# First layer of a graph network: VectorE's block in another order, and half of the products of exponentials and source rows made by GpSimd

## The chip, the cores and the metric

The kernel runs on 1 core of one Trainium2 chip. Its engines are TensorE (PE in the profile, PEld for its weight loads), VectorE (DVE), ScalarE (ACT), GpSimd (POOL) and SyncE (SP), which issues most DMAs. The metric is the device time of one execution in microseconds; less is better. A time stands for the median of several runs.

## The reference

Four graph layers follow each other on 6250 nodes of 16 features, each with a residual and a layer norm; the edges are 200,000, sorted by their target node. Only the first layer is touched by the change. For each edge and each of 16 x 16 pairs (input feature, output feature) it takes a softmax over the edges of a target, and sums the messages with it:

```
w_m = (efeat @ W_msg + b_msg).reshape(E, in_f, -1)
w_a = (efeat @ W_attn + b_attn).reshape(E, in_f, -1)
h_src = feat[src][:, :, None]
e1 = w_m * h_src
e2 = w_a * h_src
seg_max = segment_max(e2, dst)
ex = exp(e2 - seg_max[dst])
denom = segment_sum(ex, dst)
attn = ex / denom[dst]
ft = segment_sum(e1 * attn, dst)
return ft.sum(axis=1)
```

with efeat the 16 edge attributes and dst the sorted targets. Since every edge has 256 values here, this layer works on 200,704 x 256 floats (edges filled up to 128 x 1568).

## The kernel before

**Tiling.** Partition p holds the edges 1568 p to 1568 p + 1567. A block is 8 successive edges of every partition (TB0 = 8, a tile of 128 x 8 x 256), and 196 blocks follow each other (NB0 = 196). Blocks are handled in turns: `loop` writes the first turns out, then runs a hardware loop whose body holds U0 = 4 blocks (buffers b.k = 0 to 3), then writes the last ones out. Every engine has its own instruction list in an order written out by hand, and they meet through semaphores. `b.on(-1)` is the block before b; in the bodies a is b.on(-1) and c is b.on(-2), so that in one turn VectorE works on three blocks at three stages. `at(q)` puts edge q in slot 2 (q % 4) + q // 4 of a tile; a half is four slots.

**The steps of a block**, with their lines in the profile:
- GpSimd gathers the 8 source rows h of each partition, one indirect DMA for each (`gather`, L606), after SyncE has loaded the indices and the edge attributes (`load_in`, L551).
- TensorE multiplies attributes and weights: `weigh(b, half, 0)` gives w_a of a half and `weigh(b, half, 1)` w_m (L627). Each kind has one PSUM tile of a half's size, so the second half is multiplied when VectorE has read the first.
- VectorE makes e2 = w_a * h (`logits`, L702), a running maximum forward over the 8 edges (`forward`, L716) and back again (`backward`, seven steps, L724), and `factor` (L731), the logarithm of what the sums carried in from the block before are scaled by.
- TensorE puts e2 into PSUM (`put_back`, L635) and subtracts the maxima there (`less_maxima(b, n)`, n = 3 to 0, L639). Slots 4 to 7, the second half, take n = 3 and 2.
- ScalarE takes the exponentials of each half from PSUM into PX[:, 0] (`exp_half`, L680, 128x1024) and of the factor (L684).
- The product of the exponentials and h goes into PX[:, 1]. VectorE makes slots 0 to 3 with one instruction (`exp_by_source`, L740, semaphore l_t); ScalarE makes slots 4 to 7 with 64 instructions of 16 columns, each with a scale of its own (L690, semaphore l_x).
- VectorE multiplies this by w_m (`messages(b, half)`, L760), scales the sums carried in (`carried`, L750) and adds up step by step (`sum_step`, eight, L767 and L770). ST holds the denominators and numerators, and SyncE stores it and the maxima M.

**What sets the order around the change.** `weigh(c, 1, 1)` waits until `messages(c, 0)` has read the PSUM tile (semaphore l_p). TensorE does its list in order, so a's `less_maxima` that stand behind `weigh(c, 1, 1)` also wait for it. `exp_half(a, 0)` waits for `less_maxima(a, 0)`, and this for all seven `backward` steps of a. `put_back(b, n)` waits for `exp_half(a, .)`, which reads the same banks. A GpSimd gather into h[b.k] waits until the products of block b-4 have read that buffer. `search_pool` adds 49 gathers between those of the four blocks before the last four, and `search_pool_2` 49 more (L469) at the end of GpSimd's list for the layer; `search_vector_2` on VectorE waits for these.

## Time and profile before

| | us |
|---|---|
| median of 3 runs | 12024.61 |
| lowest and highest | 12020.43 and 12028.92 |
| profiled execution, its span (first to last instruction) | 11300.0 |
| VectorE busy in the span | 9347.3 (83%) |
| TensorE busy in the span | 9392.3 (83%) |
| ScalarE busy in the span | 8259.4 (73%) |
| GpSimd busy in the span | 7314.2 (65%) |

The profiled execution is known by its span alone; what a run takes outside the span (launch and end) is not in the trace, and the medians of the runs hold it. The first layer ends near 3890 us; the other three layers fill the rest. A duration in the trace is that of one instruction; where one engine's instructions overlap at their ends, the distance of two starts says what one costs.

### The profile page before, as it was taken

The page shows a single profiled execution, that of the slowest core. Times are in us where ns is not written, and L with a number is a line of the kernel's source. Part 1 is how long each engine was busy: PE and PEld are TensorE (multiplying, and loading weights), DVE is VectorE, ACT ScalarE, POOL GpSimd, SP SyncE. Part 2 cuts the span into 40 slices and gives each one's busy share as a digit, 9 for nine tenths or more (in the row PEclk, how much of TensorE's full clock was granted, in tenths as well). Part 3 has the DMA queues.
Part 4 walks back from the last instruction along what each step waited for, and adds up shares of the span by engine and source line. Part 5 has one row for each costly group of instructions (what it writes and reads, how often), then busy time and mean ns, then how long its engine had stood idle before and what let it go on. Part 6 is the DMA issues. An engine that isn't in the chain of part 4 may idle for free. (4 is left out here: it accounts for less than half of the span.)

```text
span 11300.0 us, 166457 instructions
## 1 busy us (share of the span) xinstructions
PE 9392.3 (83%) x41198; PEld 6666.9 (59%) x41198; DVE 9347.3 (83%) x14740; ACT 8259.4 (73%) x16314; POOL 7314.2 (65%) x6233
## 2 busy tenths in 40 slices
PE   5888888888888408997999488888799979988997
PEld 2333333333333206776888377777688858876886
DVE  8999999999999697886555499999587858776876
ACT  4777777777777406885888288888488848875885
POOL 4555555555555626776777677777277757776776
PEclk7666666666666559998999699999799979998998
DMA  3444444444444328886999211111299969987995
GB/s 123 178 176 176 177 178 177 176 178 178 178 178 177 126 83 293 300 304 205 287 286 287 53 48 45 46 45 45 81 331 326 330 193 328 328 288 234 330 327 190
DMA packets 756442, 2256.46 MB, mean 200 GB/s; under 512 B 278617, under 2 KB 426734, under 8 KB 679886
## 3 DMA queue, kind: packets, MB, share of 16 engines
q10 hardware_dynamic: 161280, 1027.68, 25.2%
q1 hardware_dynamic: 394718, 984.91, 25.2%
q0 software_dynamic: 200304, 242.20, 9.3%
q8 instruction: 64, 1.05, 0.0%
q14 instruction: 76, 0.62, 0.0%
HBM read 1321.84 MB, written 932.33 MB: 199 GB/s over the span
## 5 line engine op out<-in xcount | busy, mean ns | idle before, releaser
L606 POOL DMA_INDIRECT h<-in_x,idx x1568 | 2062.7, 1315 | 1672.8 <-DMA efT<-in_edge_attr_t 1236.5
L690 ACT ACTIVATE PX<-PX,h 128x16 f32<-128x16 f32 x12544 | 2509.6, 292 | 6.4
L639 PE MATMUL PS<-M,minus_ident 128*128 128x512 f32 x1568 | 1419.8, 1032 | 311.7 <-DVE M L724 311.7
L2029 PE MATMUL PS<-mhr,lhs 128*128 128x392 f32 x6272 | 1249.7, 355 | 194.9 <-DVE lhs L2193 194.9
L1996 POOL DMA_INDIRECT myg<-node_table,mix x784 | 1134.5, 1447 | 397.7 <-issue 235.7
L2092 ACT ACTIVATE mhr<-mhb 128x1568 fp32r<-128x1568 bf16 x784 | 1142.0, 1505 | 276.3 <-DVE mhb L2183 246.6
L2029 PEld LDWEIGHTS PS<-mhr,lhs 128*128 128x128 f32 x6272 | 1144.2, 192 | 276.5 <-ACT mhr L2092 217.8
L627 PE MATMUL PS<-waug,efT 17*128 17x256 f32 x6272 | 1043.1, 534 | 317.5 <-DVE e L702 291.3
L1509 PEld LDWEIGHTS PS<-every_weight,dstf 128*128 128x128 f32 x8960 | 1214.5, 190 | 137.4 <-DVE dstf L1641 38.9
L1509 PE MATMUL PS<-every_weight,dstf 128*128 128x144 f32 (+1 forms) x8960 | 1243.9, 282 | 27.3 <-DVE dstf L1641 26.9
L627 PEld LDWEIGHTS PS<-waug,efT 17*128 17x128 f32 x6272 | 612.9, 252 | 1050.5 <-issue 483.9
L770 DVE SCALAR_TENSOR_TENSOR ST<-ST,flb,PX 128x512 f32<-128x512 f32 x1372 | 1021.5, 745 | 1.4
L1560 ACT ACTIVATE r0hot<-r0hb 128x3584 fp32r<-128x3584 bf16 x224 | 716.9, 3201 | 383.5 <-DVE r0hb L1628 286.9
L1483 POOL DMA_INDIRECT c0yg<-node_table,c0ix x672 | 723.6, 1077 | 406.2 <-POOLq L1832 201.6
L680 ACT ACTIVATE PX<-PS 128x1024 f32<-128x1024 f32 x392 | 396.7, 1012 | 756.9 <-PE PS L639 756.9
L639 PEld LDWEIGHTS PS<-M,minus_ident 128*128 128x128 f32 x1568 | 397.3, 294 | 847.6 <-DVE M L724 518.5
L1483 POOL DMA_INDIRECT r0yr<-node_table,r0ix x672 | 747.1, 1112 | 230.9 <-issue 156.4
L1483 POOL DMA_INDIRECT c2yg<-node_table,c2ix x672 | 722.6, 1075 | 245.9 <-issue 185.4
L1483 POOL DMA_INDIRECT c1yg<-node_table,c1ix x672 | 720.8, 1073 | 246.6 <-issue 186.6
L1560 ACT ACTIVATE r1hot<-r1hb 128x3584 fp32r<-128x3584 bf16 x224 | 716.1, 3197 | 205.1 <-PE PS L1499 115.8
L1483 POOL DMA_INDIRECT r1yr<-node_table,r1ix x672 | 688.9, 1025 | 229.6 <-issue 182.3
L1560 ACT ACTIVATE c0hot<-c0hb 128x3584 fp32r<-128x3584 bf16 x224 | 716.3, 3199 | 135.0 <-PE PS L1499 93.3
(436 smaller groups left out, 20636.5 us busy)
## 6 DMA issues: line engine op xcount, KB each, us to landing
softmax_maxima<-M SPq DMA_DIRECT2D x196, 1024.0 KB, 3.9
softmax_denominators<-ST SPq DMA_DIRECT2D x196, 1024.0 KB
softmax_numerators<-ST SPq DMA_DIRECT2D x196, 1024.0 KB
one_hot_rows_of_sources<-r0hb ACTq DMA_DIRECT2D x224, 896.0 KB
r1hb<-one_hot_rows_of_sources ACTq DMA_DIRECT2D x224, 896.0 KB
c0hb<-one_hot_rows_of_sources ACTq DMA_DIRECT2D x224, 896.0 KB
c1hb<-one_hot_rows_of_sources ACTq DMA_DIRECT2D x224, 896.0 KB
c2hb<-one_hot_rows_of_sources ACTq DMA_DIRECT2D x224, 896.0 KB
```

Of the source, the lines that this page charges most:

```text
L606: PO.indirect_dma_start(h[b.k][:, at(q), :], None, io["x"], bass.IndirectOffsetOnAxis(ap=idx[b.k][:, q:q + 1], axis=0))\
L627: mm = PE.matmul((wm if message else wa)[:, at(q) - 4 * half, :], efT[b.k][row:row + D + 1, q // 4, :], waug[row:row + D + 1, C2 * message ...
L639: mm = PE.matmul(PS[0:CH, 4 + n, :], minus[:, :], M[b.k % 2][:, n::4, :], start=False, stop=True)
L680: S.activation(PX[b.k][:, 0, 4 * half:4 * half + 4, :], below[:, 4 * half:4 * half + 4, :], ACT.Exp).then_inc(l_ex, 1)
L690: act = S.activation(PX[b.k][:, 1, t, D * i:D * i + D], PX[b.k][:, 0, t, D * i:D * i + D], ACT.Copy, scale=h[b.k][:, t, i:i + 1])
L770: V.scalar_tensor_tensor(out=s[:, :, q, :], in0=s[:, :, q - 1, :], scalar=flb[b.k][:, q, 1:2], in1=P[:, :, at(q), :], op0=ALU.mult, op1=AL ...
L1483: PO.indirect_dma_start(to, None, table, bass.IndirectOffsetOnAxis(ap=ix[b.k][:, q:q + 1], axis=0))\
L1509: mm = PE.matmul(weighed(q)[:, r, 0:R * D], mx[q % (1 + LAG)][:, 128 * r:128 * r + 128], every[:, 0:R, :].rearrange("p r o -> p (r o)"))
L1560: S.activation(hot_[q % 2][:, :, :], hb[q // 2 if make else q % 4][:, q % 2 if make else 0, :, :], ACT.Copy)\
L1996: PO.indirect_dma_start(yg[b.k][:, q, :], None, table8, bass.IndirectOffsetOnAxis(ap=ix[b.k][:, q:q + 1], axis=0)).then_inc(m_g[b.k], 16)
L2029: mm = PE.matmul(PS[:, 6 + k, 0:A7 // 2], lhs[(G * b.k + q) % 2][:, 2 * two + r, part, :], hr[(2 * G * b.k + j) % 4][:, r, k * A7 // 2:(k ...
L2092: S.activation(hr[at_][:, :, :], hb[at_][:, :, :], ACT.Copy).then_inc(c_wd, 1)
```

## The change

VectorE's turn is written in another order: all seven backward steps of a stand in it, from its start on, where four stood at the end of the turn before; `messages(c, 0)` stands behind five of them, and `factor(a)` behind `forward(b, 0)`. `carried` moves to the turn of c. `exp_by_source` moves from VectorE to GpSimd, just ahead of the gathers into the same buffer, and makes slots 4 to 7; ScalarE's 64 products make slots 0 to 3. ScalarE takes the factor's exponential behind those of the halves. TensorE takes `less_maxima(a, 3)` behind `weigh(b, 0, 0)` and `less_maxima(a, 2)` behind `weigh(c, 1, 1)`. On GpSimd and VectorE two turns are written out ahead of the loop (head = 2).

```diff
@@ -93,13 +93,14 @@
     return not isinstance(count, int) or count > 0
 
 
-def loop(eng, body, n, tb, first=None, last=None, u=2, tail=1):
+def loop(eng, body, n, tb, first=None, last=None, u=2, head=1, tail=1):
 
     if first:
         first(Blk(0, 0, n, tb, u))
-    for k in range(u):
-        body(Blk(0, k, n, tb, u))
-    with eng.Fori(1, n // u - tail) as i:
+    for i in range(head):
+        for k in range(u):
+            body(Blk(i, k, n, tb, u))
+    with eng.Fori(head, n // u - tail) as i:
         for k in range(u):
             body(Blk(i, k, n, tb, u))
     for i in range(n // u - tail, n // u):
@@ -595,6 +596,16 @@
                 SP.wait_ge(l_ms[k], 16 * NB0 // U0)
 
         def l0_pool():
+            def exp_by_source(b):
+                P = PX[b.k]
+                PO.wait_ge(l_ex, b.count(3, 3))
+                PO.nop(nofuse=True)
+                if b.on(1).exists():
+                    PO.wait_ge(l_bw, b.on(1).count(TB0 - 1, 5))
+                PO.tensor_tensor(P[:, 1, OWN:, :].rearrange("p t (i o) -> p t i o", i=D),
+                                 P[:, 0, OWN:, :].rearrange("p t (i o) -> p t i o", i=D),
+                                 bc(h[b.k][:, OWN:, :], D, 3), ALU.mult).then_inc(l_t, 1)
+
             def gather(b):
                 PO.wait_ge(l_in[b.k], b.slot(32, 32))
                 if due(n := b.on(-U0).count(1, 1)):
@@ -609,7 +620,16 @@
                 if isinstance(b.i, int) and b.i == NB0 // U0 - 2:
                     search_pool(range(13 * b.k, min(13 * b.k + 13, JT)))
 
-            loop(PO, gather, NB0, TB0, u=U0, tail=2)
+            def body(b):
+                if b.on(-U0).exists():
+                    exp_by_source(b.on(-U0))
+                gather(b)
+
+            def last(b):
+                for n in range(1 - U0, 1):
+                    exp_by_source(b.on(n))
+
+            loop(PO, body, NB0, TB0, last=last, u=U0, head=2, tail=2)
             search_pool_2()
 
         def l0_tensor():
@@ -630,7 +650,7 @@
 
             def put_back(b, n):
                 PE.wait_ge(l_e2, b.count(2, 2 - n // 2))
-                if due(m := b.on(-1).count(3, 3 - n // 2)):
+                if due(m := b.on(-1).count(3, 2 - n // 2)):
                     PE.wait_ge(l_ex, m)
                 PE.matmul(PS[0:CH, 4 + n, :], ident[:, :], e2[:, 2 * n:2 * n + 2, :], start=True, stop=False)
 
@@ -646,14 +666,13 @@
             def body(b):
                 a = b.on(-1) if b.on(-1).exists() else None
                 c = b.on(-2) if b.on(-2).exists() else None
+                weigh(b, 0, 0)
                 if a:
                     less_maxima(a, 3)
-                weigh(b, 0, 0)
-                if a:
-                    less_maxima(a, 2)
                 if c:
                     weigh(c, 1, 1)
                 if a:
+                    less_maxima(a, 2)
                     less_maxima(a, 1)
                     less_maxima(a, 0)
                 for n in (3, 2, 1, 0):
@@ -680,12 +699,12 @@
                 S.activation(PX[b.k][:, 0, 4 * half:4 * half + 4, :], below[:, 4 * half:4 * half + 4, :], ACT.Exp).then_inc(l_ex, 1)
 
             def body(b):
+                exp_half(b, 1)
+                exp_half(b, 0)
                 S.wait_ge(l_a, b.count(1, 1))
                 S.activation(cf[b.k % 2][:, :], cf[b.k % 2][:, :], ACT.Exp).then_inc(l_ex, 1)
-                exp_half(b, 1)
-                exp_half(b, 0)
                 S.wait_ge(l_ex, b.count(3, 3))
-                for t in range(OWN, TB0):
+                for t in range(OWN):
                     for i in range(D):
                         act = S.activation(PX[b.k][:, 1, t, D * i:D * i + D], PX[b.k][:, 0, t, D * i:D * i + D], ACT.Copy,
                                            scale=h[b.k][:, t, i:i + 1])
@@ -732,19 +751,10 @@
                                        scalar=flb[b.k][:, 0, 0:1], in1=M[b.k % 2][:, 0, :],
                                        op0=ALU.add, op1=ALU.subtract).then_inc(l_a, 1)
 
-            def exp_by_source(b):
-                P = PX[b.k]
-                V.wait_ge(l_ex, b.count(3, 3))
-                if due(n := b.on(-U0).count(TB0, TB0)):
-                    V.wait_ge(l_s, n)
-                V.tensor_tensor(P[:, 1, 0:OWN, :].rearrange("p t (i o) -> p t i o", i=D),
-                                P[:, 0, 0:OWN, :].rearrange("p t (i o) -> p t i o", i=D),
-                                bc(h[b.k][:, 0:OWN, :], D, 3), ALU.mult).then_inc(l_t, 1)
-
             def carried(b):
                 if due(n := b.slot(32, 0)):
                     V.wait_ge(l_st[b.k], n)
-                V.wait_ge(l_ex, b.count(3, 1))
+                V.wait_ge(l_ex, b.count(3, 3))
                 if due(n := b.count(TB0, 0)):
                     V.wait_ge(l_s, n)
                 V.tensor_tensor(ST[b.k][:, :, 0, :], ST[(b.k - 1) % U0][:, :, TB0 - 1, :],
@@ -753,8 +763,9 @@
             def messages(b, half):
                 ts = slice(4 * half, 4 * half + 4)
                 P = PX[b.k]
-                V.wait_ge(l_t, b.count(1, 1))
                 if half:
+                    V.wait_ge(l_t, b.count(1, 1))
+                else:
                     V.wait_ge(l_x, b.count(1, 1))
                 V.wait_ge(l_wm, b.count(2, half + 1))
                 V.tensor_tensor(P[:, 1, ts, :], wm[:, :, :], P[:, 1, ts, :], ALU.mult).then_inc(l_p, 1)
@@ -776,20 +787,28 @@
                 a = b.on(-1) if b.on(-1).exists() else None
                 c = b.on(-2) if b.on(-2).exists() else None
                 if a:
+                    backward(a, 0)
+                if c:
+                    carried(c)
+                if a:
+                    backward(a, 1)
+                logits(b, 1)
+                if a:
+                    backward(a, 2)
+                    backward(a, 3)
                     backward(a, 4)
-                logits(b, 1)
+                if c:
+                    messages(c, 0)
+                logits(b, 0)
                 if a:
                     backward(a, 5)
                 if c:
-                    messages(c, 0)
+                    sum_step(c, 0)
                 if a:
                     backward(a, 6)
-                logits(b, 0)
+                forward(b, 0)
                 if a:
                     factor(a)
-                if c:
-                    sum_step(c, 0)
-                forward(b, 0)
                 if c:
                     sum_step(c, 1)
                 forward(b, 1)
@@ -799,24 +818,17 @@
                     forward(b, q)
                     if c:
                         sum_step(c, q)
-                backward(b, 0)
-                if a:
-                    carried(a)
-                backward(b, 1)
-                backward(b, 2)
-                backward(b, 3)
-                if a:
-                    exp_by_source(a)
                 if isinstance(b.i, int) and b.i == NB0 // U0 - 1 and b.k == 0:
                     search_vector()
 
             def last(b):
-                for n in (4, 5, 6):
+                backward(b, 0)
+                carried(b.on(-1))
+                for n in range(1, TB0 - 1):
                     backward(b, n)
                 factor(b)
                 for c in (b.on(-1), b):
                     if c.k == b.k:
-                        exp_by_source(c)
                         carried(c)
                     messages(c, 0)
                     sum_step(c, 0)
@@ -825,7 +837,7 @@
                     for q in range(2, TB0):
                         sum_step(c, q)
 
-            loop(V, body, NB0, TB0, last=last, u=U0, tail=1)
+            loop(V, body, NB0, TB0, last=last, u=U0, head=2, tail=1)
             search_vector_2()
 
         l0_first_vector()
```

VectorE, one turn inside the written-out start (M is the maxima, e the logits e2, PS PSUM, PX the exponentials and products, ST the sums, cf the factor). Before:

```order
L740 TENSOR_TENSOR PX<-PX,h 128x1024 [waits l_ex]
L724 SCALAR_TENSOR_TENSOR M<-M,flb 128x256 [waits l_bw,l_fw]
L702 TENSOR_TENSOR e<-PS,h 128x1024 [waits l_wa,l_g3]
L724 SCALAR_TENSOR_TENSOR M<-M,flb 128x256 [waits l_bw,l_fw]
L760 TENSOR_TENSOR PX<-PS,PX 128x1024 [waits l_wm,l_t]
L724 SCALAR_TENSOR_TENSOR M<-M,flb 128x256 [waits l_bw,l_fw]
L702 TENSOR_TENSOR e<-PS,h 128x1024 [waits l_wa]
L731 SCALAR_TENSOR_TENSOR cf<-M,flb 128x256 [waits l_q,l_bw]
L767 TENSOR_TENSOR ST<-ST,PX 128x2x256 [waits l_q,l_p]
L716 SCALAR_TENSOR_TENSOR M<-M,flb,e 128x256 [waits l_ms1,l_fw,l_e2,l_fl3]
L770 SCALAR_TENSOR_TENSOR ST<-ST,flb,PX 128x2x256 [waits l_s,l_p]
...
L760 TENSOR_TENSOR PX<-PS,PX 128x1024 [waits l_wm,l_x,l_t]
```

The same turn after (L743 is backward, L721 logits, L771 messages, L760 carried, L735 forward, L750 factor, L778 and L781 the sums):

```order
L743 SCALAR_TENSOR_TENSOR M<-M,flb 128x256 [waits l_bw,l_fw]
L721 TENSOR_TENSOR e<-PS,h 128x1024 [waits l_wa,l_g3]
L743 SCALAR_TENSOR_TENSOR M<-M,flb 128x256 [waits l_bw,l_fw] x3
L771 TENSOR_TENSOR PX<-PS,PX 128x1024 [waits l_wm,l_x]
L721 TENSOR_TENSOR e<-PS,h 128x1024 [waits l_wa]
L743 SCALAR_TENSOR_TENSOR M<-M,flb 128x256 [waits l_bw,l_fw]
L778 TENSOR_TENSOR ST<-ST,PX 128x2x256 [waits l_q,l_p]
L743 SCALAR_TENSOR_TENSOR M<-M,flb 128x256 [waits l_bw,l_fw]
L735 SCALAR_TENSOR_TENSOR M<-M,flb,e 128x256 [waits l_ms1,l_fw,l_e2,l_fl3]
L750 SCALAR_TENSOR_TENSOR cf<-M,flb 128x256 [waits l_q,l_bw]
...
L771 TENSOR_TENSOR PX<-PS,PX 128x1024 [waits l_wm,l_t]
```

The wait on l_x, ScalarE's products, has moved from the second messages of a turn to the first, and the product L740 is gone from VectorE.

TensorE in the written-out start, one turn (L627 is weigh, L639 less_maxima, L635 put_back). Before:

```order
L639 MATMUL PS<-M,minus_ident 128x512 [waits l_bw]
L627 MATMUL PS<-waug,efT 128x256 [waits l_e2,l_in3]
L627 MATMUL PS<-waug,efT 128x256 x3
L639 MATMUL PS<-M,minus_ident 128x512 [waits l_bw]
L627 MATMUL PS<-waug,efT 128x256 [waits l_p]
L627 MATMUL PS<-waug,efT 128x256 x3
L639 MATMUL PS<-M,minus_ident 128x512 [waits l_bw] x2
L635 MATMUL PS<-e,ident 128x512 [waits l_ex,l_e2] x4
```

After (L647, L659 and L655):

```order
L647 MATMUL PS<-waug,efT 128x256 [waits l_e2,l_in3]
L647 MATMUL PS<-waug,efT 128x256 x3
L659 MATMUL PS<-M,minus_ident 128x512 [waits l_bw]
L647 MATMUL PS<-waug,efT 128x256 [waits l_p]
L647 MATMUL PS<-waug,efT 128x256 x3
L659 MATMUL PS<-M,minus_ident 128x512 [waits l_bw] x3
L655 MATMUL PS<-e,ident 128x512 [waits l_ex,l_e2] x4
```

Behind the weigh that waits on l_p three less_maxima stand now, where two stood.

## Rows read from the trace of the kernel before

**Rows 1.** Page, VectorE's tenths; window, busy us of PE, PEld, DVE, ACT, POOL, clock.
```profile
DVE  8999999999999697886555499999587858776876
...
1000.00:3000.00 2000.00, 1704.29 (x5062) 738.71 (x5063) 1925.30 (x3165) 1585.58 (x7063) 1117.63 (x842) 0.68 0.48 177
```

**Rows 2.** Instructions of line L740: count, duration min/median/max, first and last start.
```profile
L740 DVE TENSOR_TENSOR PX<-PX,h x196: 1209/1217/1225, 124.9 to 3859.4; 128x1024 f32<-128x1024 f32 x196
```

**Rows 3.** Timeline of VectorE: start us, duration us, instruction; two blocks far apart.
```profile
504.58 1.22 DVE L740 TENSOR_TENSOR PX<-PX,h 128x1024 f32<-128x1024 f32 x1
...
3499.93 1.22 DVE L740 TENSOR_TENSOR PX<-PX,h 128x1024 f32<-128x1024 f32 x1
```

**Rows 4.** Timeline of VectorE in one block; in brackets the idle time before.
```profile
2003.83 1.21 DVE L702 TENSOR_TENSOR e<-PS,h 128x1024 f32<-128x1024 f32 x1
...
2005.36 1.21 DVE L760 TENSOR_TENSOR PX<-PS,PX 128x1024 f32<-128x1024 f32 x1
2006.49 0.47 DVE L724 SCALAR_TENSOR_TENSOR M<-M,flb 128x256 f32<-128x256 f32 x1
2007.22 1.23 DVE L702 TENSOR_TENSOR e<-PS,h 128x1024 f32<-128x1024 f32 x1 [0.26 <-PE PS L627]
2008.36 0.48 DVE L731 SCALAR_TENSOR_TENSOR cf<-M,flb 128x256 f32<-128x256 f32 x1
2008.76 0.68 DVE L767 TENSOR_TENSOR ST<-ST,PX 128x512 f32<-128x512 f32 x1
...
2011.23 1.23 DVE L760 TENSOR_TENSOR PX<-PS,PX 128x1024 f32<-128x1024 f32 x1 [0.34 <-PE PS L627]
```

**Rows 5.** Timeline of TensorE in the same block and into the next.
```profile
2005.10 2.08 PE L627 MATMUL PS<-waug,efT 17*128 17x256 f32 x8 [1.59 <-DVE e L702]
2007.10 2.08 PE L639 MATMUL PS<-M,minus_ident 128*128 128x512 f32 x2
2009.11 2.08 PE L627 MATMUL PS<-waug,efT 17*128 17x256 f32 x8
2011.12 3.78 PE L639 MATMUL PS<-M,minus_ident 128*128 128x512 f32 x4
2014.69 3.75 PE L635 MATMUL PS<-e,ident 128*128 128x512 f32 x8
...
2030.02 3.78 PE L639 MATMUL PS<-M,minus_ident 128*128 128x512 f32 x4
```

**Rows 6.** Timeline of ScalarE in the same block.
```profile
2009.80 0.40 ACT L684 ACTIVATE cf<-cf 128x256 f32<-128x256 f32 x1
...
2014.94 1.02 ACT L680 ACTIVATE PX<-PS 128x1024 f32<-128x1024 f32 x1 [3.84 <-PE PS L639]
2015.99 12.80 ACT L690 ACTIVATE PX<-PX,h 128x16 f32<-128x16 f32 x64
```

**Rows 7.** Windows of 0.9 us; granted clock third from the end (PEclk).
```profile
2014.40:2015.30 0.90, 0.90 (x3) 0.36 (x2) 0.90 (x3) 0.36 (x1) 0.28 (x1) 0.67 0.92 391
...
2035.10:2036.00 0.90, 0.90 (x3) 0.45 (x2) 0.90 (x2) 0.90 (x6) 0.86 (x1) 0.79 0.49 155
```

**Rows 8.** Timeline of GpSimd, first and last of eight gathers; two other operations by line.
```profile
2015.02 1.43 POOL L606 DMA_INDIRECT h<-in_x,idx  x1 [5.36 <-DMA efT<-in_edge_attr_t]
...
2027.36 0.94 POOL L606 DMA_INDIRECT h<-in_x,idx  x1 [0.30 <-issue]
...
L1939 POOL IOTA iob<- 128x784 int16 x1 | 0.8, 782 | 0.0
...
L281 POOL TENSOR_SCALAR_AFFINE_SELECT tn<-tn 128x128 f32<-128x128 f32 x1 | 0.3, 289 | 0.0
```

**Rows 9.** End of the layer: L469's gathers by line; VectorE's timeline.
```profile
L469 POOL DMA_INDIRECT lasts_got<-in_dst,search_at x49: 943/947/4532, 3814.0 to 3885.0; - x49
...
3861.11 1.22 DVE L760 TENSOR_TENSOR PX<-PS,PX 128x1024 f32<-128x1024 f32 x1
...
3887.29 1.79 DVE L489 TENSOR_TENSOR lasts_got<-lasts_got,tn 128x1568 f32<-128x1568 int32 x1 [13.85 <-DMA lasts_got<-in_dst,search_at]
```

## The prediction, made before the changed kernel ran

> **What bounds the kernel now.** I read the page's row of busy tenths first: VectorE stands at 9 in the first fourteen slices of forty, which are the first layer [rows 1]. The change touches nothing else. Then the period: VectorE's product L740 runs once per block, 196 times [rows 2]; from its start at 504.58 to its start at 3499.93 us there are 158 blocks, so one block takes 2995.35 / 158 = 18.96 us [rows 3]. From 1000 to 3000 us VectorE is busy for 1925 of 2000 us [rows 1]; the idle times that recur in a block are 0.26 and 0.34 us, both ahead of a product that reads a PSUM tile of TensorE [rows 4]. VectorE is thus the bound, and its instructions fill the block.
>
> The timelines of ScalarE and TensorE show how near the next bound is. What follows names, in VectorE's turn for block b, a = b-1 and c = b-2, as the code does. From the start of messages(c, 0) at 2005.36 [rows 4] the chain goes: weigh(c, 1, 1) on TensorE at 2009.11, which must overwrite the PSUM tile that messages(c, 0) has read; less_maxima(a, 1) and (a, 0) from 2011.12 [rows 5]; the exponentials of a's first half at 2014.94; 64 small products from 2015.99, which last 12.80 us and end at 2028.79 [rows 6]. In the kernel before these products belong to the second half and are wanted by messages(a, 1), at about 2030.2 (one period after the 2011.23 of [rows 4]). So a chain of 23.4 us ends 1.4 us before it is needed, because its consumer comes 5.87 us (2011.23 - 2005.36) later in the turn than the instruction that starts it. I rest the forecast on this number.
>
> **What the change does, part by part.**
>
> 1. VectorE loses L740. Its duration is 1.217 us [rows 2], of which about 1.13 us count, as a product of that size lets the next instruction start 1.13 us after it (2005.36 to 2006.49, [rows 4]). Worth 1.13 us per block while VectorE is the bound: 196 x 1.13 = 221 us. The rest of VectorE's list has the same instructions. The new order also puts three steps of the backward pass and messages(c, 0) between logits(b, 1) and logits(b, 0), and this removes the wait of 0.26 us; the 0.34 goes too, as more work stands between the two messages.
>
> 2. ScalarE makes the products of the first half (t = 0 to 3) in place of the second. Same count, 64 of 128x16, same 12.80 us. But now messages(c, 0) waits for them, and messages(c, 0) itself starts the chain that leads to the next ones. The cover of 5.87 us is gone: the chain closes on itself in one turn, and its length is a lower bound of the period, whatever VectorE saves.
>
> 3. TensorE: weigh(b, 0, 0) goes ahead of less_maxima(a, 3), which is harmless, as both are done while the chain is elsewhere. less_maxima(a, 2), which stood ahead of weigh(c, 1, 1), goes behind it, so that the chain holds three of these matmuls where it held two.
>
> 4. The length of the new chain, from the start of messages(c, 0), with TensorE at 1.2 GHz:
> to the start of weigh(c, 1, 1) 1.27 us (2003.83 to 2005.10, a VectorE product of that size and the matmuls that wait for it, [rows 4, 5]);
> weigh to the first less_maxima 2.01 (2009.11 to 2011.12, [rows 5]);
> one more less_maxima 1.71: the two at 2011.12 hold four records, and their ends let the next group start 3.57 us later at 2014.69, which with the switch of weights is 0.86 for each of the two records of one [rows 5];
> the last two, to the start of the exponentials 3.82 (2011.12 to 2014.94, [rows 5, 6]);
> the exponentials 1.0 (1.05 to the next start), then the carried factor's exponential, which now stands here, 0.40, and 0.05 for the wait on its completion [rows 6];
> 64 products 12.80 [rows 6];
> back to VectorE 0.07, taken as the 0.06 from the end of a VectorE instruction at 2005.04 to TensorE's start at 2005.10.
> Sum 1.27 + 2.01 + 1.71 + 3.82 + 1.45 + 12.80 + 0.07 = 23.13 us.
> It does not help that backward(a, 6) is early enough: after messages(c, 0) come logits 1.14, backward 0.40 (the distance that steps of 256 elements have, 2008.36 to 2008.76), the first sum 0.68 and backward(a, 6) 0.48 [rows 4], so it ends at 1.13 + 2.70 = 3.83 us at the latest, well ahead of the last less_maxima.
>
> 5. TensorE's clock. The granted clock is 0.50 (1.2 GHz) at the weigh, less_maxima and weigh of [rows 5], and becomes 1.00 (2.4 GHz) at about 2015.0 in one block and 2035.5 in the next [rows 7], 3.9 and 5.5 us after the starts of the L639 groups at 2011.12 and 2030.02 [rows 5]. Before 2005.10 TensorE had been idle for 1.59 us [rows 5]. In the new kernel it is idle for some 5 us ahead of weigh(c, 1, 1), since VectorE is standing at messages(c, 0) and weigh(b, 0, 0) and less_maxima(a, 3) are long done; so I let the chain start at 1.2 GHz. The first less_maxima of the chain starts 3.28 us after messages(c, 0) and the last ends at 8.4. A rise as far behind the group's start as in the rows, 3.9 to 5.5 us, comes at 7.2 to 8.8 and saves between 0.6 and nothing; a rise 3.9 us behind the start of weigh, the earliest I allow, comes at 5.2 and saves 1.6. I take 0.4, near the rows: a period of 22.7 us.
>
> 6. VectorE's new slack: its work per turn is 18.96 - 1.13 - 0.6 = 17.2 us, so it waits some 5.5 us at messages(c, 0) in every turn.
>
> 7. GpSimd makes the second half's products (128x1024, two inputs), ahead of the eight gathers of the same buffer. No row shows such an operation there. From below: an IOTA of 784 elements, which only writes, takes 782 ns, about 1.0 us for 1024; from above: AFFINE_SELECT takes 289 ns for 128, 2.3 us for 1024 with one input, and twice that, 4.6 us, for two [rows 8]. I take 2.3. The queue: gathers begin 3.8 us after weigh(c, 1, 1) ends (2011.19 to 2015.02) and last 13.3 us (to 2028.3) [rows 5, 8]. In the new turn that is 7.1 to 20.4 us after messages(c, 0); the product comes next, 20.4 to 22.7 (25.0 at 4.6 us), and messages(c, 1) wants it 5.5 us into the next turn, at 28.2. Cost 0 at either end, and if the period were 19 us instead of 22.7 it would just be in time at 24.5.
> The Trainium skill (SBUF — State Buffer, Who interferes with whom) has a rule that speaks against this part: a VectorE instruction with two SBUF inputs and a GpSimd instruction that reads SBUF exclude each other for their whole length. No run here shows it yet. By it up to one whole GpSimd product is added to a turn that VectorE fills; in my turn the product falls into VectorE's wait, so the rule leaves the sum as it is. The skill (GPSIMD Engine Reference, Performance versus the Vector engine) gives 4497 ns for a two-input operation of 2048 elements, an estimate of 2.25 us here.
>
> 8. The end of the layer. The 49 gathers of L469, 3814.0 to 3885.0 us, run beside the last blocks, and VectorE then waits 13.85 us for the last of them, until 3887.29, which is 26.2 us after the last block's messages at 3861.11 [rows 9]. In the changed kernel they stand behind the last GpSimd product on the same queue. That product can start 12.9 us before the last messages(c, 0) and takes 2.3; the gathers and the landing take 73.3 (3814.0 to 3887.29). So L489 starts 73.3 - 10.6 = 62.7 us after, 36.5 us later than now. The 49 gathers of L462 delay blocks near the end in both kernels; I take no difference (within 20 us).
>
> **Sum.** 195 steps from the first messages to the last: 195 x (22.7 - 18.96) = 729; with the end 36: 766 us. The profiled span is 11300.0 us and the median of the runs 12024.6; the 724.6 us between them lie outside the span, and I leave them as they are. Forecast 12024.6 + 766 = 12790 us, a span of about 12065.
>
> **Rivals.**
> TensorE keeps 2.4 GHz in the chain. For: it has 1.00 at the end of each block. Against: the idle time ahead of weigh(c, 1, 1). weigh then costs 1.0 and each less_maxima 0.86, half of rows 5's; exponentials start at 5.2 us, and the period is 5.2 + 1.45 + 12.80 + 0.07 = 19.5: 195 x 0.54 + 36 = 141, 12166 us. Still slower.
> VectorE blocked by GpSimd. The chain does not bind, VectorE does, at 18.96 - 1.13 = 17.8, and every GpSimd product of 2.3 us holds it up: 20.1 us a turn, 195 x 1.14 + 36 = 258, 12283 us. This decides from a GpSimd product over 1.1 us, with VectorE busy beside it. It would be the mechanism of the skill's rule in 7. Against: VectorE would have to be fully busy, which the chain forbids.
> Faster: ScalarE's products are in time. VectorE's work of 17.2 us is then the period: 195 x -1.73 + 36 = -301, 11724 us. It decides where the exponentials of a's first half start less than 17.2 - 14.3 = 2.9 us after messages(c, 0). Against: backward(a, 6), which they need, ends only at 3.8. It would need that I have the order of two waits wrong.
>
> **Chances and range.** The forecast 0.83, TensorE at 2.4 GHz 0.06, VectorE blocked 0.04, faster 0.05, nothing that shows 0.02. Within the forecast's case: 23.13 us throughout gives 195 x 4.17 + 36 = 849, 12874 us, and 0.2 us more per turn in handovers 12913; the earliest rise allowed in 5 gives 21.5, 12557, and 0.2 us less 12520. The range 12520 to 12910 leaves out the four other cases, 0.17, and little else. Faster by over 0.2% has 0.05, within 0.2% (what a measurement of this kernel can tell from no change) 0.02, slower 0.93.
>
> **What would show it.** In the changed profile VectorE's first-half messages should wait about 5 us per block for ScalarE's small products, about 1 ms in total, and VectorE's busy share in the first layer should fall from 0.96 to under 0.8. ScalarE should show its 64 products back to back, with idle time only before the exponentials. The layer should end some 760 us later, near 4660 us. GpSimd's product should take 1 to 4.6 us and nobody should wait for it but at the end of the loop. The forecast is wrong if VectorE waits for GpSimd or for nothing, or if TensorE's clock in the chain is 1.00.

## The result, and the profile after

The changed kernel takes 12745.06 us (median of 4 runs, 12734.93 to 12745.4), the kernel before 12025.28 us beside it: a ratio of 1.0594, 95% interval 1.0581 to 1.0607. It is 720 us slower.

The page of the changed kernel: VectorE's and ScalarE's busy tenths, the clock granted to TensorE and GB/s moved, in 40 slices of the span.

```profile
span 12744.1 us, 166431 instructions
...
DVE  6777777777777668777455469999576647665665
ACT  3666666666666521777477548888477747765774
...
PEclk7666666666666656999899879999799979998997
...
GB/s 100 150 148 151 151 148 148 150 149 148 152 150 148 134 106 140 274 275 268 166 250 248 187 48 45 46 44 46 78 293 293 289 169 294 291 254 204 294 289 167
```

VectorE stood at 9 in the first layer [rows 1] and stands at 7; no engine has taken its place. The window of the same stretch, its columns as in [rows 1]:

```profile
1000.00:3000.00 2000.00, 1351.70 (x4248) 599.55 (x4249) 1508.59 (x2574) 1343.87 (x5944) 1319.37 (x801) 0.68 0.40 149
```

VectorE is busy for 1509 us where it was for 1925. When nobody is busy all the time, something goes in a circle. What the messages waited for, over the whole layer:

```profile
L771 DVE TENSOR_TENSOR PX<-PS,PX x392: 1207/1224/1226, 153.5 to 4581.1; 128x1024 f32<-128x1024 f32 x196
its engine sat idle before it (us, times) until:
  ACT PX L709: 849.2, 157
  issue: 232.9, 37
  POOL PX L605: 12.4, 1
```

1095 us of waiting, 849 of it for ScalarE's small products, once a turn; 37 waits of the same size (233 us) stand without a releaser. From the start of one messages(c, 0) at 490.90 to one at 3487.40 us there are 133 turns, 22.53 us each (18.96 before). The circle in two successive turns, first VectorE (L771 after a wait is messages(c, 0)), then TensorE (L647 weigh, L659 less_maxima, L655 put_back), then ScalarE (L699 exponentials, L709 products):

```profile
2001.02 1.23 DVE L771 TENSOR_TENSOR PX<-PS,PX 128x1024 f32<-128x1024 f32 x1 [6.07 <-ACT PX L709]
...
2006.53 1.22 DVE L771 TENSOR_TENSOR PX<-PS,PX 128x1024 f32<-128x1024 f32 x1
...
2023.13 1.23 DVE L771 TENSOR_TENSOR PX<-PS,PX 128x1024 f32<-128x1024 f32 x1 [5.07 <-ACT PX L709]
...
2046.05 1.22 DVE L771 TENSOR_TENSOR PX<-PS,PX 128x1024 f32<-128x1024 f32 x1 [5.87 <-ACT PX L709]
```

```profile
2002.30 2.07 PE L647 MATMUL PS<-waug,efT 17*128 17x256 f32 x8 [5.05 <-DVE PX L771]
2004.30 4.50 PE L659 MATMUL PS<-M,minus_ident 128*128 128x512 f32 x6
2008.65 3.60 PE L655 MATMUL PS<-e,ident 128*128 128x512 f32 x8
...
2024.41 2.08 PE L647 MATMUL PS<-waug,efT 17*128 17x256 f32 x8 [4.74 <-DVE PX L771]
2026.42 5.39 PE L659 MATMUL PS<-M,minus_ident 128*128 128x512 f32 x6
2031.65 3.60 PE L655 MATMUL PS<-e,ident 128*128 128x512 f32 x8
```

```profile
2008.85 1.02 ACT L699 ACTIVATE PX<-PS 128x1024 f32<-128x1024 f32 x1 [1.33 <-PE PS L659]
2009.77 0.41 ACT L705 ACTIVATE cf<-cf 128x256 f32<-128x256 f32 x1
2010.21 12.81 ACT L709 ACTIVATE PX<-PX,h 128x16 f32<-128x16 f32 x64
...
2031.85 1.02 ACT L699 ACTIVATE PX<-PS 128x1024 f32<-128x1024 f32 x1 [2.19 <-PE PS L659]
```

Read as a sum for the first turn: 1.28 (2001.02 to 2002.30), 2.00, 4.55 to the exponentials, 1.36, 12.81, 0.11 back to VectorE at 2023.13: 22.11 us. The second turn is 22.92, and the difference is the less_maxima: 5.43 to the exponentials. What parts them is when the granted clock (third number from the end, as in [rows 7]) rises:

```profile
2007.00:2007.90 0.90, 0.90 (x3) 0.45 (x2) 0.90 (x2) 0.52 (x1) 0.00 (x0) 0.62 0.80 302
2007.90:2008.80 0.90, 0.90 (x4) 0.42 (x3) 0.90 (x3) 0.00 (x0) 0.68 (x1) 1.00 1.05 437
...
2030.00:2030.90 0.90, 0.90 (x3) 0.38 (x2) 0.90 (x3) 0.00 (x0) 0.65 (x1) 0.50 0.94 391
```

```profile
2030.90:2031.80 0.90, 0.90 (x3) 0.44 (x2) 0.90 (x3) 0.00 (x0) 0.88 (x1) 0.62 1.06 437
```

The clock is 0.50 (1.2 GHz) until about 2007.7 in the first turn, 6.7 us after messages(c, 0), and until about 2031.6 in the second, 8.5 us after; behind that it is 1.00 (2.4 GHz). Where in a window it rises is worked out from the window's mean, 0.62. GpSimd's part, the last of a set of gathers and the product, and the end of the layer on VectorE, which answers to [rows 9]:

```profile
2008.12 1.54 POOL L617 DMA_INDIRECT h<-in_x,idx  x1 [5.86 <-DMA efT<-in_edge_attr_t]
...
2022.47 0.95 POOL L617 DMA_INDIRECT h<-in_x,idx  x1 [0.30 <-issue]
2023.44 1.94 POOL L605 TENSOR_TENSOR PX<-PX,h 128x1024 f32<-128x1024 f32 x1
```

```profile
4632.45 1.79 DVE L490 TENSOR_TENSOR lasts_got<-lasts_got,tn 128x1568 f32<-128x1568 int32 x1 [45.10 <-DMA lasts_got<-in_dst,search_at]
```

The layer ends at 4638.5 us (begin_idx and end_idx, the last two instructions of the layer on VectorE), 745 us later than the 3893.3 us of the profile before.

### The profile page after: what moved, and what is told of

It reads as the page before. It is cut to its first block and busy times, and to the rows that moved or that the text cites. A ratio compares the mean times of both kernels' runs of the same rounds, so it can differ in the third digit from the quotient of the medians.

```text
span 12744.1 us, 166431 instructions
## 1 busy us (share of the span) xinstructions
PE 9465.7 (74%) x41198; PEld 6738.7 (53%) x41198; DVE 9049.5 (71%) x14544; ACT 8294.2 (65%) x16314; POOL 8138.3 (64%) x6429
## 5 line engine op out<-in xcount | busy, mean ns | idle before, releaser
L617 POOL DMA_INDIRECT h<-in_x,idx x1568 | 2517.1, 1605 | 1540.1 <-DMA efT<-in_edge_attr_t 1101.6
L709 ACT ACTIVATE PX<-PX,h 128x16 f32<-128x16 f32 x12544 | 2511.5, 292 | 16.5 <-issue 10.0
L647 PE MATMUL PS<-waug,efT 17*128 17x256 f32 x6272 | 985.4, 512 | 1490.5 <-DVE PX L771 865.5
L647 PEld LDWEIGHTS PS<-waug,efT 17*128 17x128 f32 x6272 | 574.8, 237 | 2086.0 <-DVE PX L771 1165.9
L1521 PE MATMUL PS<-every_weight,dstf 128*128 128x144 f32 (+1 forms) x8960 | 1281.3, 286 | 205.7 <-DVE dstf L1653 165.0
L659 PE MATMUL PS<-M,minus_ident 128*128 128x512 f32 x1568 | 1373.1, 1026 | 13.4 <-DVE M L743 13.3
L699 ACT ACTIVATE PX<-PS 128x1024 f32<-128x1024 f32 x392 | 401.0, 1023 | 1500.3 <-PE PS L659 1299.4
L771 DVE TENSOR_TENSOR PX<-PS,PX 128x1024 f32<-128x1024 f32 x392 | 478.5, 1221 | 1095.5 <-ACT PX L709 849.2
L781 DVE SCALAR_TENSOR_TENSOR ST<-ST,flb,PX 128x512 f32<-128x512 f32 x1372 | 1021.8, 745 | 1.3
```

The source lines that it names most:

```text
L617: PO.indirect_dma_start(h[b.k][:, at(q), :], None, io["x"], bass.IndirectOffsetOnAxis(ap=idx[b.k][:, q:q + 1], axis=0))\
L647: mm = PE.matmul((wm if message else wa)[:, at(q) - 4 * half, :], efT[b.k][row:row + D + 1, q // 4, :], waug[row:row + D + 1, C2 * message ...
L659: mm = PE.matmul(PS[0:CH, 4 + n, :], minus[:, :], M[b.k % 2][:, n::4, :], start=False, stop=True)
L709: act = S.activation(PX[b.k][:, 1, t, D * i:D * i + D], PX[b.k][:, 0, t, D * i:D * i + D], ACT.Copy, scale=h[b.k][:, t, i:i + 1])
L771: V.tensor_tensor(P[:, 1, ts, :], wm[:, :, :], P[:, 1, ts, :], ALU.mult).then_inc(l_p, 1)
L781: V.scalar_tensor_tensor(out=s[:, :, q, :], in0=s[:, :, q - 1, :], scalar=flb[b.k][:, q, 1:2], in1=P[:, :, at(q), :], op0=ALU.mult, op1=AL ...
```

## The experiments

The theory is the prediction's: ScalarE's products went to the half that is wanted first, so the chain of L771, weigh, less_maxima, exponentials and products closes in one turn. Its rivals: the new order of VectorE costs the time; GpSimd's product does, by a wait or by holding VectorE up. The runs were made on three chips, on which the kernel before takes 12095.84 us (the first four), 11300.45 us (the next four) and 12035.38 and 12028.49 us (the last three); each ratio is against the kernel before on the same chip. "Layer end" is where begin_idx is made in the profile, and "turn" the mean distance between the starts of first-half messages from 1000 to 3000 us: 18.96 us in the kernel before, 22.53 in the changed one.

**1. The kernel before again (before_again).**

> The kernel before, unchanged, for its profile. The profiled execution of it read so far has a span of 11300.0 us where the runs take 12025; the changed kernel's has 12744.1 where the runs take 12745, so what lies outside a span is about 1 us and the 724.6 us cannot be that. Theory: that one execution ran its three later layers faster (7407 us from the end of the first layer to the end, against 8105 in the changed kernel, with the same instructions), and the first layer as usual. Then this profile has a span near 12024, a first layer that ends near 3893, and 8130 us after it. Rival: the first layer too is slower in ordinary runs, and ends near 3950 to 4100; then the step from 18.96 us per block was measured against the wrong base.

Measured: 12099.25 us, span 12098.0, turn 18.96, layer end 3913.2. The part of a run outside the span is 1.25 us. The first layer is as in the profile before; the three others take 8185 us where they took 7407. So the 724.6 us of the prediction are no time outside the span: the profile had been taken in an execution whose later layers were faster. The first messages come at 135.96 us here and at 128.00 in the profile before, so the start of the layer differs by 8 us between two executions of one kernel.

**2. The new order alone (order_alone).** VectorE, TensorE and ScalarE have the orders of the changed kernel; L740 is back on VectorE, now ahead of messages(c, 0), and ScalarE keeps the second half (the waits of `messages` follow, which the cut does not show):

```diff
-                for t in range(OWN):
+                for t in range(OWN, TB0):
...
                 if c:
+                    exp_by_source(c)
                     messages(c, 0)
```

> The changed kernel's orders of VectorE, TensorE and ScalarE, but VectorE makes the first half's product again, just ahead of messages(c, 0), ScalarE the second half's, GpSimd none. Theory (the chain from messages(c, 0) through TensorE and ScalarE's 64 products back to messages(c, 0) sets 22.7 us per block): ScalarE's products are wanted 5.5 us later in the turn again, the chain asks for 23.1 - 5.5 = 17.6 us, VectorE's own work of about 18.4 us binds, 195 x (18.4 - 18.96) = -110 us: 11915, between 11850 and 12030. Rival (VectorE's new order itself costs, by waits on TensorE): over 12300.

Measured: 11981.0 us (11954.52 to 11991.13), ratio 0.9904 (0.9888 to 0.9921), 115 us faster than before; turn 18.28, layer end 3799.6. VectorE is busy for all but 17 us and waits for no one:

```profile
1000.00:3000.00 2000.00, 1655.08 (x5251) 741.95 (x5252) 1983.33 (x3282) 1660.51 (x7347) 1452.52 (x879) 0.72 0.50 184
```

The new orders cost nothing; they give 0.68 us a turn. By the ratios, 0.9904 against 1.0594, this kernel beats both.

**3. Two less_maxima behind the weigh instead of three (subtract2_first).** Against the changed kernel:

```diff
+                if a:
+                    less_maxima(a, 2)
                 if c:
                     weigh(c, 1, 1)
                 if a:
-                    less_maxima(a, 2)
                     less_maxima(a, 1)
```

> The changed kernel with less_maxima(a, 2) back ahead of weigh(c, 1, 1). Theory: the chain is shorter by one less_maxima, 0.86 us at 2.4 GHz or 1.71 at 1.2 GHz, and nothing else binds: 195 x 0.86 to 1.71 = 168 to 333 us less than 12745, 12412 to 12577 us. Rival (VectorE waits for GpSimd or for gathers, not for that chain): 12745, no change.

Measured: 12503.84 us (12485.94 to 12516.01), ratio 1.0329 (1.0312 to 1.0347); layer end 4336.4, 302 us earlier than in the changed kernel; turn 20.89, shorter by 1.64. The instruction lies on the circle.

**4. Half of ScalarE's products left out (half_products).** ScalarE makes 32 of its 64; the others stay at the zero they are set to once at the start, in this run and in the others that leave products out (the cuts do not show it). Against the changed kernel:

```diff
-                    for i in range(D):
+                    for i in range(D // 2):
```

> The changed kernel with 32 of ScalarE's 64 small products left out in each block (input features 8 to 15 of the first half; their places are set to 0 once at the start, 7 us). Theory: the chain falls by 6.4 us to 16.3, VectorE's 17.2 us of work bind: 12025 + 195 x (17.2 - 18.96) + 36 + 7 = 11725 us if GpSimd's product, which now falls beside VectorE's work, costs VectorE nothing; if it holds VectorE for its whole 1.94 us, 19.1 us per block and 12095 us. Rival (ScalarE's products do not set the period): 12745.

Measured: 12194.86 us (12184.52 to 12201.26), ratio 1.0077 (1.006 to 1.0093); layer end 4016.1, 622 us earlier than in the changed kernel. VectorE is busy for 1965 of 2000 us, and yet the turn is 19.24 us, with less work on VectorE than in run 2. GpSimd's product is why. VectorE's instructions of over 1.3 us, and GpSimd's product beside them:

```profile
1999.46 2.81 DVE L780 TENSOR_TENSOR ST<-ST,PX 128x512 f32<-128x512 f32 x1
...
1999.77 1.94 POOL L607 TENSOR_TENSOR PX<-PX,h 128x1024 f32<-128x1024 f32 x1
```

```profile
2019.54 2.79 DVE L737 SCALAR_TENSOR_TENSOR M<-M,flb,e 128x256 f32<-128x256 f32 x1
```

L780 takes 0.68 us and L737 0.48 us elsewhere: each is stretched by 2.1 to 2.3 us and ends 0.3 to 0.6 us after GpSimd's product, which runs to 2001.71 and, for the second, from 2020.10 to 2022.04. By the means of the layer L737 takes 676 ns (475 in run 5) and L780 911 (683): 8 x 0.201 + 0.228 = 1.8 us a turn.

**5. GpSimd's product shrunk to 16 columns (gpsimd_16).** Against the changed kernel, 1008 of the 1024 columns of the second half are left out:

```diff
-                PO.tensor_tensor(P[:, 1, OWN:, :] ...
+                PO.tensor_tensor(P[:, 1, OWN, 0:D], P[:, 0, OWN, 0:D], h[b.k][:, OWN, :], ALU.mult).then_inc(l_t, 1)
```

> The changed kernel with GpSimd's product cut from 1024 columns to 16 per block (the rest of the second half keeps the 0 it is set to at the start, 7 us). Theory: GpSimd's product is on no path while VectorE waits for ScalarE, so the block keeps its 22.7 us: the first layer ends near 4638 us in the profile as in the changed kernel, up to 15 us earlier by the end of the queue. Rival (GpSimd's 1.94 us hold VectorE in the changed kernel): 1.94 x 195 = 378 us less.

Measured: 12026.73 us (12022.54 to 12034.48), ratio 1.0644 (1.0627 to 1.0662); layer end 4611.2, 27 us earlier; the turn is 22.53 us to the hundredth, as in the changed kernel. A product of 0.23 us in place of 1.94 changes nothing in a turn: GpSimd's operation is off the path of the changed kernel. Of the 27 us, 19 lie ahead of the first messages (134.16 us for 153.47); from the first to the last of them the two kernels differ by 8 us in 4424.

**6. Both left out (half_and_16).** Runs 4 and 5 in one.

> Both left out: 32 of ScalarE's 64 products and all but 16 columns of GpSimd's. Beside half_products (first layer ends at 4016 us, one VectorE instruction per block stretched from 0.48 or 0.68 to 2.8 us while GpSimd's product runs) it prices that stretch. Theory (the two engines exclude each other on reads, 2.3 us per block): the block falls from 19.3 to 17.2 us, the first layer ends 195 x 2.1 = 410 us earlier, near 3610. Rival (the stretch is hidden by TensorE, whose waits appear in its place): the end moves by less than 100 us.

Measured: 11147.27 us, ratio 0.9867 (0.985 to 0.9883); layer end 3735.4, 281 us earlier than in run 4, where 410 were expected. The turn is 17.92 us: with the circle short, GpSimd's product does cost time, 19.24 - 17.92 = 1.32 us. The rest of the expectation went into a new wait, on VectorE in the window of 1000 to 3000 us (us in total, times, longest):

```profile
DVE PX L771 <- POOL PX L607: 60.2, 56, 1.4
DVE PX L771 <- ACT PX L709: 21.7, 44, 0.7
```

**7. GpSimd's product in the order of before (gpsimd_between).** The kernel before, with L740 moved to GpSimd between the fourth and fifth gather; ScalarE keeps the second half:

```diff
+                    if q == 3 and b.on(-3).exists():
+                        exp_by_source(b.on(-3))
```

> The kernel before with one part of the change alone: VectorE's product of the first half goes to GpSimd, between the fourth and fifth gather of a later block; all orders as before. VectorE loses 1.13 us per block. Theory of exclusion: GpSimd's product falls beside VectorE's two-input steps and costs them 2.3 us, net 195 x 1.2 = 230 us slower than before at most, 0 to 230 us slower, plus some 30 us at the end of the layer. Rival (no cost to VectorE): 195 x 1.13 to 1.7 = 220 to 330 us faster.

Measured: 11519.44 us, ratio 1.0194 (1.0177 to 1.0211), 219 us slower than before; layer end 4108.2, turn 19.88. Two costs, of which one was not expected: L738 (backward) takes 674 ns on average for 484 before, 7 x 0.19 = 1.3 us a turn, and VectorE waits for the product, which comes late behind gathers:

```profile
2009.06 1.23 DVE L765 TENSOR_TENSOR PX<-PS,PX 128x1024 f32<-128x1024 f32 x1 [3.35 <-POOL PX L602]
```

**8. 56 products instead of 64 (products_56).** Eight of ScalarE's 64 are left out and stay zero; against the changed kernel `range(D)` becomes `range(D - 2)`.

> The changed kernel with 8 of ScalarE's 64 small products left out (input features 14 and 15 of the first half; 7 us of clearing at the start). Theory: the chain binds one to one, 8 x 0.2 = 1.6 us per block and 195 x 1.6 = 312 us less than the changed kernel, 305 with the clearing; the clock of TensorE may shift this by 60 us. Rival (something else stands just behind the chain): less than 150 us.

Measured: 11652.54 us, ratio 1.0313 (1.0296 to 1.033); layer end 4237.6, 401 us earlier than in the changed kernel, where 305 were expected, give or take 60; turn 20.48, shorter by 2.05 us for 1.6 us of products. The circle shrinks with ScalarE's count. The surplus is in the less_maxima: from 1000 to 3000 us their groups of six records last 4.48 us on average (4.30 to 4.53), where the changed kernel's last 4.95 (4.14 to 5.49). In two successive turns here the granted clock rises 6.6 and 6.7 us after messages(c, 0), not 6.7 and 8.5.

**9. The halves exchanged (swap_halves).** The changed kernel, with GpSimd's product for the first half, in the same place on its queue but without its wait on the backward pass, and ScalarE's for the second (the waits of `messages` are exchanged too, outside the cut):

```diff
-                PO.tensor_tensor(P[:, 1, OWN:, :] ...
+                PO.tensor_tensor(P[:, 1, 0:OWN, :] ...
...
-                for t in range(OWN):
+                for t in range(OWN, TB0):
```

> The changed kernel, with the two engines' halves exchanged: GpSimd makes the products of the first half, in the same place ahead of the gathers and without its wait on the backward pass, ScalarE the 64 of the second half. Theory (ScalarE's chain closed on itself because its products went to the first half): with them in the second half the chain has its cover of 5.9 us again. But GpSimd's product now stands right ahead of the first messages, behind eight gathers that weigh(c, 1, 1) lets start, so a second chain closes: 1.3 + 2.0 + 3.9 us to the first gather, 10 to 13.3 for the eight, 1.9 for the product, 0.1: 19.2 to 22.5, I say 20.9 us a block against 22.67. That is 195 x 1.8 = 350 us below the changed kernel, with 30 us either way for each 0.15 us of gathers; VectorE waits for GpSimd's product at its first messages and no longer for ScalarE. Rival (GpSimd's operation or the new order of VectorE costs the time, whichever half ScalarE makes): the block stays at 22.7 us and VectorE still waits for ScalarE's small products.

Measured: 13104.84 us (13101.48 to 13119.02), ratio 1.0894 (1.0876 to 1.0912); layer end 5004.6, turn 24.36. The wait for ScalarE is gone, as the theory has it, and the second circle closes, as it has it too; its length was wrong by 3.5 us. VectorE and GpSimd in one turn:

```profile
2001.53 1.23 DVE L769 TENSOR_TENSOR PX<-PS,PX 128x1024 f32<-128x1024 f32 x1 [7.36 <-POOL PX L603]
...
2025.92 1.22 DVE L769 TENSOR_TENSOR PX<-PS,PX 128x1024 f32<-128x1024 f32 x1 [7.36 <-POOL PX L603]
```

```profile
2008.68 1.49 POOL L615 DMA_INDIRECT h<-in_x,idx  x1 [7.18 <-DMA efT<-in_edge_attr_t]
2010.48 5.95 POOL L615 DMA_INDIRECT h<-in_x,idx  x1 [0.31 <-issue]
...
2023.95 1.94 POOL L603 TENSOR_TENSOR PX<-PX,h 128x1024 f32<-128x1024 f32 x1
```

7.15 us to the first gather, 15.27 for the eight, 1.94 and 0.03: 24.39 us in this turn. I had allowed 10 to 13.3 for the eight; one gather of 5.95 us stands among them (see the last section).

**10. The halves exchanged, product between the gathers (swap_between).** As 9, with the product behind the fourth gather, as in run 7.

> The same exchange of halves, with GpSimd's product between the fourth and the fifth gather of the next buffer but two, so that it starts after four gathers. Theory: neither chain closes below 17 us, VectorE's own work of 17.3 us and about 2 us of every GpSimd product (2.1 to 2.3 with half of ScalarE's products left out) fill the turn: 19.4 us, 195 x 3.3 = 640 us below the changed kernel, about 80 above the kernel before (0 to 200 above, more where gathers come late). Rival (the changed kernel's loss is not ScalarE's chain): within 100 us of the changed kernel.

Measured: 12153.88 us (12144.5 to 12167.32), ratio 1.0098 (1.0081 to 1.0115), 118 us slower than before; layer end 4053.3, 585 us earlier than in the changed kernel, turn 19.42. Nothing was left out here, VectorE's order and its saved L740 are those of the changed kernel, and ScalarE makes the same 64 products. Only who makes which half is exchanged, and where GpSimd does it: about four fifths of the loss are gone. But the 2.3 us a turn above VectorE's own work are not the lengthened VectorE instructions that I expected. VectorE is busy for 1766 of 2000 us and waits for GpSimd:

```profile
2025.70 1.23 DVE L766 TENSOR_TENSOR PX<-PS,PX 128x1024 f32<-128x1024 f32 x1 [2.36 <-POOL PX L603]
```

**11. The product behind the first gather (swap_early).**

```diff
-                    if q == 3 and b.on(-3).exists():
+                    if q == 0 and b.on(-3).exists():
```

> As the last but one run, with GpSimd's product behind the first gather of a set instead of the fourth. The exponentials it needs end about 9.5 us after the first messages, one gather ends at 8.7, so it runs at about 9.6 to 11.6, beside VectorE's steps that read two tiles of SBUF, and long before the next first messages want it. The wait of 2.35 us for GpSimd goes. Theory (the two engines exclude each other while VectorE reads two tiles of SBUF): the 1.94 us come back as a lengthened VectorE instruction, VectorE's 17.2 us become 19.2, and the time is within 60 us of the last but one run's 12154, that is 60 to 180 above the kernel before, with VectorE busy for over 1900 of 2000 us. Rival (only the wait counted): VectorE's turn is 17.2 us, GpSimd's own turn of eight gathers and a product, 17.8 us, sets the period, and the time is 195 x 1.1 = 220 us below the kernel before, with VectorE busy for 1930 at most and no instruction over 1.3 us in it.

Measured: 12028.61 us (12018.86 to 12044.11), ratio 1.0004 (0.9994 to 1.0014); layer end 3921.1, turn 18.77. Between the theory and its rival, and outside the 60 us that the theory allowed: the wait is gone and the stretched instructions have come, but smaller than foreseen. VectorE and GpSimd:

```profile
2012.56 2.36 DVE L738 SCALAR_TENSOR_TENSOR M<-M,flb 128x256 f32<-128x256 f32 x3
...
2025.81 2.42 DVE L776 SCALAR_TENSOR_TENSOR ST<-ST,flb,PX 128x512 f32<-128x512 f32 x1
```

```profile
2011.65 1.94 POOL L603 TENSOR_TENSOR PX<-PX,h 128x1024 f32<-128x1024 f32 x1
...
2025.41 2.28 POOL L603 TENSOR_TENSOR PX<-PX,h 128x1024 f32<-128x1024 f32 x1 [1.21 <-ACT cf L700]
```

Three L738 take 1.51 us undisturbed, L776 0.74: 0.85 us lost in the first pair, 1.68 in the second. By the means of the layer L776 takes 797 ns (741 in run 10), L730 525 (473) and L738 543 (497): 7 x 0.056 + 8 x 0.052 + 7 x 0.046 = 1.13 us a turn. That is what L740 had cost. Where the first part of GpSimd's product falls on L716, which reads a PSUM tile and h (2011.42 to 2012.6 in the first pair), VectorE goes on beside it.

## Why the prediction was right

**The mechanism (steps 2 and 6): shown.** L771 waits 5 to 6 us a turn for L709, where 5.5 were said; VectorE's busy share of the window is 0.75, under the 0.8. In addition ScalarE's count moves the turn (run 8), the matmul behind the weigh does (run 3), and giving ScalarE the later half again makes VectorE's wait for it vanish (runs 9 and 10).

**The period (steps 3 to 5): 22.53 us measured, 22.7 predicted.** Term by term in the turns shown: 1.28 for 1.27, 2.00 for 2.01, the three less_maxima 4.55 and 5.43 for 5.53, 1.36 for 1.45, 12.81 for 12.80, 0.11 for 0.07. In the mean of the two turns the clock saves 0.54 us (4.99 for 5.53) where 0.4 was allowed, and the exponentials take 0.09 less; these two make the 0.2. (Step 4 counts a record at 0.86 us, where a quarter of its 3.57 us is 0.89.) The rise comes 6.7 and 8.5 us after messages(c, 0), where 7.2 to 8.8 had been read off [rows 5, 7], so it saves up to 1 us in one turn and almost nothing in the next.

**VectorE's saving (step 1): right, and not used.** The two waits that the new order was to remove, 0.6 us a turn, are gone in run 2, which gains 0.68. Without L740 VectorE's work is 1766 / 2000 x 19.42 = 17.1 us a turn (run 10), for the 17.2 of step 6. It would be worth 1.13 us a turn only in a kernel in which VectorE sets the period, and there the product comes back as stretched instructions (runs 4 and 11).

**GpSimd's product (step 7): 1.94 us, predicted 2.3, cost 0.** Its queue was read rightly: the product starts at 2023.44, behind the last gather, and messages(c, 1) comes at 2028.65. Run 5 bounds its cost at 27 us in the layer, and at 8 us from the first messages on. The Trainium skill (SBUF — State Buffer, Who interferes with whom) has VectorE instructions with two SBUF inputs and GpSimd instructions that read SBUF exclude each other; runs 4, 7 and 11 agree, with VectorE's lengthened by up to 2.3 us beside a product of 1.94. In the changed kernel the product falls on VectorE's wait, on L771 and on L721, which read a PSUM tile, and L781 takes 745 ns as L770 did before.

**The end (step 8): 29 us for 36.** L490 waits 45.10 us where L489 waited 13.85 and starts 54.9 us behind the last messages(c, 0), at 4577.59, for 26.2 before [rows 9]. The gathers and the landing take 64.9 us (4567.6 to 4632.45), not 73.3.

**What was wrong: small terms of the sum.** The first layer grew by 745 us between the two profiles, for 766 in the sum. The 195 turns give 195 x (22.53 - 18.96) = 696 for 729. The blocks near the end that wait for the search's gathers (turns of up to 31.1 us before and 33.3 after) lose 37 us before and 31 after, so "I take no difference" holds to 5 us. A term that I did not have is the start: the first messages come at 153.47 us for 128.00. How much of these 25 us the change makes is open: they come at 135.96 in run 1, which is the kernel before, and at 134.16 in run 5, which has the changed kernel's order. With the end: 696 - 5 + 25 + 29 = 745.

The sentence on the 724.6 us that "lie outside the span" was false: 1.2 us do (12744.1 and 12745.34 in the changed kernel's profiled run), and run 1 shows the rest to be the later layers of another execution. So the span came out at 12744.1 us, and not at the 12065 forecast. For the time it did no harm, as the first layer ends at nearly the same time in both (3893.3 and 3913.2) and the change is an absolute number of microseconds. The runs differ by 720 us, 25 less than the profiles' first layers, of which 20 are the difference of these two ends.

**The rivals.** TensorE at 2.4 GHz in the whole circle: refuted by the 0.50 of the windows. VectorE blocked by GpSimd: not here, but it is what runs 4 and 11 became once the circle was short. Faster: VectorE's own 17.1 us were not reached by any run that made all products; the nearest full kernel is run 2, 18.28 us, in which VectorE keeps L740.

## What to carry to other kernels

Before work is moved off the bound engine, follow the chain that its consumer starts, through every in-order queue, back to that same consumer; if it closes within one turn, its length is the new period, and the cover that it had before is the number to look at (here 5.9 us, the distance between the first and the second messages). Give the slow producer the half that is wanted last, and place a helper's operation where its queue is sure to be there in time (run 10 against run 9: 950 us). A VectorE product handed to GpSimd was worth nothing in the best placement found (run 11, 1.0004, turn 18.77 us); the new orders without it were worth 1% (run 2, 18.28 us).

## What the runs showed that I had not expected

- The same kernel before takes 11300.45, 12095.84 and about 12030 us on three chips, and its first layer ends within 20 us in the two profiles at hand (3893.3 and 3913.2). The 778 us lie in the three later layers, whose slices move up to 331 GB/s in the one profile and up to 292 in the other. Why, no run shows. That profiled execution had a span (11300.0 us) and a mean granted clock (0.837) like the runs on the chip of 11300.45 us, while the runs on the two others have 0.825 to 0.830. A span and a median may come from different chips; only the ratio of runs on one chip compares kernels.
- The traces point to VectorE as what holds up GpSimd's gathers. From 1000 to 3000 us one gather of every set of eight lasts long in the changed kernel, 5.8 us on average where the others mostly take 0.94 to 1.5, and the set takes 15.1 us; in the kernel before about half of the sets have one, of 4.0 us on average, and a set takes 12.8. The long one ends at a fixed place in VectorE's list. In the changed kernel that is 0.49 to 0.52 us after the start of L721, which reads a PSUM tile and stands behind nearly 8 us of VectorE instructions with two SBUF inputs, in all 89 sets; run 2 has the same in 110. In the kernel before it is 9.37 to 9.40 us after the second messages, among the backward steps, in all 57. One set of the changed kernel, GpSimd and VectorE:

```profile
2032.08 5.95 POOL L617 DMA_INDIRECT h<-in_x,idx  x1 [0.30 <-issue]
```

```profile
2037.13 0.48 DVE L743 SCALAR_TENSOR_TENSOR M<-M,flb 128x256 f32<-128x256 f32 x1
2037.52 1.22 DVE L721 TENSOR_TENSOR e<-PS,h 128x1024 f32<-128x1024 f32 x1
```

  Run 2 has the long gathers without any product on GpSimd, and run 7 has them in the order of before (6.0 us on average), so neither explains them alone. What differs in the turns shown is where a set starts: 7.1 us after messages(c, 0) in the changed kernel, 9.7 in the kernel before. By this reading a part of VectorE's wait for GpSimd in runs 9 and 10 is of VectorE's own making; run 9 came out some 360 us slower than the changed kernel where 350 us faster had been expected. It is read from the ends of the gathers alone; no run was made to test it.
- Eight small products of 0.2 us fewer gave 2.05 us a turn (run 8), as the granted clock rises early in each of its turns. Why it does so there, no run shows.
